# Mixture-of-experts stage of a fused attention and expert layer: another order of shared units, zero rows, gathers and down rows

## The reference, cut to what matters

```python
scores = softmax(xt @ gate_w.T)                       # 8 experts
idx = top_k(scores + gate_b, 2)[1]
cw = sum(one_hot(idx, 8) * weights[..., None], axis=1)
h1 = einsum('td,efd->etf', xt, w1) + b1[:, None, :]
h3 = einsum('td,efd->etf', xt, w3) + b3[:, None, :]
y = einsum('etf,edf->etd', swiglu(h1 * h3), w2) + b2[:, None, :]
routed = einsum('te,etd->td', cw, y)
shared = swiglu((xt @ sw1.T + sb1) * (xt @ sw3.T + sb3)) @ sw2.T + sb2
return routed + shared
```

## Time and profile before

| | us |
|---|---|
| median of 3 runs | 1384.94 |
| lowest and highest | 1378.19, 1387.31 |
| the profiled execution's own time | 1380.67 |
| its span | 1378.8 |
| mean granted TensorE clock | 0.909 |
| attention | 0 to about 980 |
| experts | about 980 to 1378.8 |

### The profile page before, as it was taken

One profiled execution on the slowest core, in us unless ns is written; L12 is line 12 of the kernel. 1 busy time (PEld: TensorE's weight loads), 2 busy tenths in 40 slices (PEclk: granted clock), 3 DMA queues, 4 the chain that ended last, 5 costly groups with the idle time before them and its releaser, 6 DMA issues. The chain is left out here.

```text
span 1378.8 us, 22331 instructions
## 1 busy us (share of the span) xinstructions
PE 1133.1 (82%) x6568; PEld 475.6 (34%) x6568; DVE 1094.1 (79%) x2499; ACT 943.7 (68%) x1748; POOL 833.1 (60%) x1129
## 2 busy tenths in 40 slices
PE   2599999999998998999999899984599987887710
PEld 0122222232232232222222222222478866665510
DVE  2589999999999899989899998933567755999734
ACT  1028888787786886877778678783489975777511
POOL 5254366565675776667567575556378525887555
PEclk9559999999998999999899999997699998999955
DMA  2361242242241431423323224002224443444312
GB/s 65 82 187 50 56 102 63 50 109 55 65 117 40 104 87 51 112 56 79 78 63 102 70 58 110 19 26 91 68 87 153 146 145 108 138 135 144 95 33 76
DMA packets 104009, 119.89 MB, mean 87 GB/s; under 512 B 13217, under 2 KB 80965, under 8 KB 103621
## 3 DMA queue, kind: packets, MB, share of 16 engines
q1 hardware_dynamic: 93728, 97.55, 26.2%
q0 software_dynamic: 8192, 16.79, 4.4%
q10 hardware_dynamic: 1968, 4.13, 0.8%
HBM read 58.91 MB, written 59.51 MB: 86 GB/s over the span
## 5 line engine op out<-in xcount | busy, mean ns | idle before, releaser
L929 DVE TENSOR_REDUCE MX<-psS 128x1 f32<-128x512 f32 x1024 | 652.9, 679 | 71.5 <-PE psS L423 62.7
L678 ACT ACTIVATE PR<-psST 128x512 f32<-128x512 f32 x986 | 536.8, 600 | 166.0 <-PE psST L411 153.2
L423 PE MATMUL psS<-KS,QS 48*128 48x512 bf16 x1024 | 368.0, 408 | 51.9 <-DVE MX L929 27.2
L411 PE MATMUL psST<-QS,KS 51*128 51x512 bf16 x986 | 337.2, 393 | 22.0 <-ACT PR L678 8.1
L437 PE MATMUL psPV<-PR,V 128*32 128x512 f32 x2048 | 283.0, 625 | 7.1 <-ACT OT L592 2.0
L411 PEld LDWEIGHTS psST<-QS,KS 51*128 51x128 bf16 x986 | 76.4, 93 | 382.3 <-ACT PR L678 323.7
L1703 POOL DMA_INDIRECT GOT<-scratch_y,FROM x128 | 128.8, 1007 | 38.4 <-issue 35.9
L423 PEld LDWEIGHTS psS<-KS,QS 48*128 48x128 bf16 x1024 | 84.5, 94 | 114.0 <-DVE MX L929 87.9
L1033 POOL DMA_INDIRECT scratch_x<-XN,POSI x96 | 95.3, 993 | 27.8 <-issue 27.4
L1060 POOL TENSOR_TENSOR ROT<-ROT,RES 128x512 f32<-128x512 f32 x32 | 40.5, 1267 | 91.2 <-DVE RES L737 91.2
L1378 PE MATMUL psH<-XH,WS 128*128 128x512 f32 x184 | 82.5, 448 | 10.3 <-DVE XL L1532 7.6
(11 more groups left out here) (173 smaller groups left out, 2016.7 us busy)
## 6 DMA issues: line engine op xcount, KB each, us to landing
scratch_parts<-PT SPq DMA_DIRECT2D x192, 128.0 KB
QS<-scratch_parts SPq DMA_DIRECT2D x64, 192.0 KB, 3.4
KS<-scratch_parts SPq DMA_DIRECT2D x64, 192.0 KB, 4.5
XR<-scratch_x SPq DMA_DIRECT2D x46, 256.0 KB
scratch_y<-YR SPq DMA_DIRECT2D x46, 256.0 KB
scratch_x<-ZERO SPq DMA_DIRECT2D x18, 256.0 KB
X<-in_x SPq DMA_DIRECT2D x16, 256.0 KB, 4.9
scratch_turned<-XT SPq DMA_DIRECT2D x16, 256.0 KB, 4.6
```

The costliest lines, as they stand in the source:

```text
L411: nc.tensor.matmul(bank(st_banks(t), k)[:], KS[t.par][rows, h // 2, kc * P:(kc + 1) * P], QS[t.par][rows, h // 2, :], start=True, stop=Tru ...
L423: nc.tensor.matmul(bank(psS, k)[:], QS[b.par][rows, h // 2, qc * P:(qc + 1) * P], KS[b.par][rows, h // 2, :], start=True, stop=True).then_ ...
L678: nc.scalar.activation(PR[:, s % 2, j, :], bank(st_banks(t), k)[:], ACT.Exp, scale=SCALE).then_inc(st_exp, 1)
L929: nc.vector.tensor_reduce(out=MX[:, qc, h:h + 1], in_=bank(psS, k)[:], axis=AX.X, op=ALU.max).then_inc(s_max, 1)
```

## The change

1. **Order.** Stream two carries a shared unit only after its third, sixth and ninth routed unit (`MIXED` = 3: S4 to S6 in slots 34, 38 and 42). R45 moves from slot 55 to slot 52, and nine shared units S7 to S15 fill slots 53 to 61. `GATHER_AT` of stream two becomes slot 56. `FINISH` is 37, 39, ... 49 for batches 0 to 6 and 56, 58, 60, 62, ... 72 for batches 7 to 15.
2. **Zero rows.** The eight tiles are written one at a time at slots 0, 3, ... 21, ahead of the slot's store, and no longer wait for stream two's scatters.
3. **Down rows.** POOL's copy of 128x132 is gone; SP copies the same rows from WD to DS by a DMA (`load_down(p + 2)`, between `store_rows(p - 2)` and `load(p + 3)`), with a register load of the expert's number, for each of the 46 routed units. PE and ACT wait for its landing.
4. **POOL.** `rsqrt` of a finished batch comes between the second and the third gather of its slot.
5. **Buffers and slots.** YR gets three buffers instead of two, R(b) twelve instead of eight (the third four are XN2). `shift` and `scale` come at +4, `residual` at +6 and ahead of `weigh`, `store_out` at +7.

```diff
-        R_BUFS = 2 * QC
+        R_BUFS = 3 * QC
+        MIXED = 3
+        Y_BUFS = 3
...
-            if i % 3 == 2:
+            if i % 3 == 2 and i < 3 * MIXED:
                 ORDER.append(("S", next(shared)))
...
-        FINISH = [GATHER_AT[int(b >= SPAN)] + (GATHERS * (b - FIRST_B[int(b >= SPAN)] + 1)) // PACE + 1 for b in range(B)]
-        END = max(FINISH) + 6
+        FINISH = []
+        for b in range(B):
+            st = int(b >= SPAN)
+            soonest = GATHER_AT[st] + GATHERS * (b - FIRST_B[st] + 1) // PACE + 1
+            FINISH.append(max(soonest, SLOT_S[b] + LAG + 1, FINISH[-1] + 2 if b else 0))
+        END = max(FINISH) + 8
...
+            def load_down(i):
+
+                if i == 0:
+                    sp.wait_ge(halved, 1)
+                if i in FIRST_UNIT:
+                    sp.wait_ge(expert_ready, FIRST_UNIT.index(i) + 1)
+                if i >= D_BUFS:
+                    sp.wait_ge(y_psum, SLOT_R[i - D_BUFS] + 1)
+                    sp.wait_ge(gl_ready, 2 * (SLOT_R[i - D_BUFS] + 1))
+                e = sp.value_load(EXPERT[0:1, i:i + 1], min_val=0, max_val=NE)
+                sp.dma_start(DS[:, i % D_BUFS], WD[:, bass.ds(e, 1)].rearrange("p e c -> p (e c)")
+                             ).then_inc(down_loaded[i % D_BUFS], 16)
+
...
-            def zero_tails():
-                for i in range(4):
-                    sp.wait_ge(scattered[i], SCATTERED[1][i] * 16 * GATHERS)
-                sp.wait_ge(count_ready, 1)
-                for e in range(NE):
-                    row = sp.value_load(CNTI[0:1, e:e + 1], min_val=ROOM * e, max_val=ROOM * e + SPAN * N)
...
+            def zero_tail(e):
+                if e == 0:
+                    sp.wait_ge(count_ready, 1)
+                row = sp.value_load(CNTI[0:1, e:e + 1], min_val=ROOM * e, max_val=ROOM * e + SPAN * N)
...
             for p in range(END):
-                if p == SLOT_R[UNITS[0]] - 6:
-                    zero_tails()
+                if p % 3 == 0 and p // 3 < NE:
+                    zero_tail(p // 3)
                 if routed(p - LAG):
                     store_rows(p - LAG)
+                if routed(p + 2):
+                    load_down(ORDER[p + 2][1])
                 load(p + 3)
-                if p - 6 in FINISH:
-                    store_out(FINISH.index(p - 6))
-            store_out(B - 1)
+                if p - 7 in FINISH:
+                    store_out(FINISH.index(p - 7))
...
                 if routed(p):
-                    pe.wait_ge(ds_ready, ORDER[p][1] + 1)
+                    pe.wait_ge(down_loaded[ORDER[p][1] % D_BUFS], 16 * (ORDER[p][1] // D_BUFS + 1))
...
                 if routed(p):
-                    if i >= 2:
-                        act.wait_ge(y_stored[i % 2], 16 * (i // 2))
-                    place = YR[:, i % 2]
+                    if i >= Y_BUFS:
+                        act.wait_ge(y_stored[i % Y_BUFS], 16 * (i // Y_BUFS))
+                    place = YR[:, i % Y_BUFS]
...
-                if p - 3 in FINISH:
-                    scale(FINISH.index(p - 3))
+                if p - 4 in FINISH:
+                    scale(FINISH.index(p - 4))
...
+                if p - 6 in FINISH:
+                    residual(FINISH.index(p - 6))
                 if p in FINISH:
                     weigh(FINISH.index(p))
-                if p - 5 in FINISH:
-                    residual(FINISH.index(p - 5))
...
-            def stage(i):
...
-                nc.gpsimd.tensor_copy(DS[:, i % D_BUFS], WD[:, bass.ds(e, 1)].rearrange("p e c -> p (e c)")).then_inc(ds_ready, 1)
...
+            def gathers(p, first, last):
+                for st in range(STREAMS):
+                    n = PACE * (p - GATHER_AT[st])
+                    if 0 <= n < (SPAN, B - SPAN)[st] * GATHERS:
+                        for i in range(first, last):
+                            gather(FIRST_B[st] * GATHERS + n + i)
...
-                if routed(p + 2):
-                    stage(ORDER[p + 2][1])
...
+                gathers(p, 0, PACE // 2)
                 if p - 2 in FINISH:
                     rsqrt(FINISH.index(p - 2))
+                gathers(p, PACE // 2, PACE)
```

More of the change, by code:

```diff
@@ L1208, in experts @@
         HA = sb("HA", [P, HA_BUFS, N], F32)
-        YR = sb("YR", [P, 2, QC, C], F32)
+        YR = sb("YR", [P, Y_BUFS, QC, C], F32)
         GOT = sb("GOT", [P, G_BUFS, TOPK, QC, C], F32)
@@ L1241, in experts @@
         y_psum, y_evicted = sem("y_psum"), sem("y_evicted")
-        y_stored = [sem(f"y_stored{i}") for i in range(2)]
-        ws_act, ds_ready = sem("staged_by_act"), sem("down_staged")
+        y_stored = [sem(f"y_stored{i}") for i in range(Y_BUFS)]
+        ws_act, down_loaded = sem("staged_by_act"), [sem(f"down_loaded{i}") for i in range(D_BUFS)]
         gathered = [sem(f"gathered{i}") for i in range(G_BUFS)]
@@ L1251, in R @@
         def R(b):
+            if b % R_BUFS >= 2 * QC:
+                return XN2[:, b % QC]
             half = (W1, W3)[b % R_BUFS // QC][:].rearrange("p e f -> p (e f)")
@@ L1287, in load_rows @@
                     "(p q) c -> p q c", q=QC)).then_inc(xr_loaded[i % X_BUFS], 16)
-            def zero_tails():
-                for i in range(4):
-                    sp.wait_ge(scattered[i], SCATTERED[1][i] * 16 * GATHERS)
-                sp.wait_ge(count_ready, 1)
-                for e in range(NE):
-                    row = sp.value_load(CNTI[0:1, e:e + 1], min_val=ROOM * e, max_val=ROOM * e + SPAN * N)
-                    sp.dma_start(XG[1][bass.ds(row, TILE), :].rearrange("(p q) c -> p q c", q=QC),
-                                 ZERO[:].rearrange("p (q c) -> p q c", q=QC)).then_inc(zero_filled, 16)
+            def zero_tail(e):
+                if e == 0:
+                    sp.wait_ge(count_ready, 1)
+                row = sp.value_load(CNTI[0:1, e:e + 1], min_val=ROOM * e, max_val=ROOM * e + SPAN * N)
+                sp.dma_start(XG[1][bass.ds(row, TILE), :].rearrange("(p q) c -> p q c", q=QC),
+                             ZERO[:].rearrange("p (q c) -> p q c", q=QC)).then_inc(zero_filled, 16)
             def load_turned(b):
@@ L1439, in hidden @@
                 if gl == 0 and routed(p):
-                    act.wait_ge(ds_ready, ORDER[p][1] + 1)
+                    act.wait_ge(down_loaded[ORDER[p][1] % D_BUFS], 16 * (ORDER[p][1] // D_BUFS + 1))
                 if due(2 * p + gl - 3):
@@ L1455, in evict @@
                 if routed(p):
-                    if i >= 2:
-                        act.wait_ge(y_stored[i % 2], 16 * (i // 2))
-                    place = YR[:, i % 2]
+                    if i >= Y_BUFS:
+                        act.wait_ge(y_stored[i % Y_BUFS], 16 * (i // Y_BUFS))
+                    place = YR[:, i % Y_BUFS]
                 else:
-                    if i < R_BUFS:
+                    if i < 2 * QC:
                         act.wait_ge(split, min(2 * (i % QC) + 3, EXP_ALL))
+                    elif i < R_BUFS:
+                        act.wait_ge(scattered[i % QC], SCATTERED[1][i % QC] * 16 * GATHERS)
                     else:
@@ L1635, in _ @@
                         clip(p, 0)
-                if p - 3 in FINISH:
-                    shift(FINISH.index(p - 3))
+                if p - 4 in FINISH:
+                    shift(FINISH.index(p - 4))
                 if 0 <= p - 1 < ALL:
@@ L1698, in gather @@
                     pool.wait_ge(from_step, 4 * (st + 1))
-                    for i in range(2):
-                        pool.wait_ge(y_stored[i], 16 * ((FIRST_UNIT[st] + UNITS[st] + 1 - i) // 2))
+                    for i in range(Y_BUFS):
+                        pool.wait_ge(y_stored[i], 16 * len(range(i, FIRST_UNIT[st] + UNITS[st], Y_BUFS)))
                 if rest == 0 and b >= G_BUFS:
@@ L1725, in _ @@
                     scatter(2 * p + 1)
-                for st in range(STREAMS):
-                    for n in range(PACE * (p - GATHER_AT[st]), PACE * (p - GATHER_AT[st] + 1)):
-                        if 0 <= n < (SPAN, B - SPAN)[st] * GATHERS:
-                            gather(FIRST_B[st] * GATHERS + n)
+                gathers(p, 0, PACE // 2)
                 if p - 2 in FINISH:
                     rsqrt(FINISH.index(p - 2))
+                gathers(p, PACE // 2, PACE)
 def build(nc, x, wqkvT, chan, ones, cos, sin, perm, ident, table, count, gate_wT, gate_b, w1T, w3T, wdT, b2, out):
```

8 lines of the change are left out of this document (1 added, 7 removed).

## The result

The changed kernel took 1399.68 us in the median of four runs (1397.55 to 1404.26), beside 1384.25 us (1378.19 to 1387.31) of the kernel before. The ratio is 1.0106, with a 95% interval from 1.0062 to 1.015. The forecast was 1357: the sign was wrong. Ratios and intervals leave out disturbed runs, one of e7 (1716.48 us) and the two longest of e17.

A forecast was written before the change was run, and what follows sets the result against it. PE was taken to bound stream one, DVE's list batches 0 to 6, POOL's 48 gathers the end. Zero rows -8.3, down rows +4, batch 10's gathers from 1271.5, plus 67.4, 16.5 and 1.9 around the span: 1357 us, range 1336 to 1377.

The forecast's parts named there:

- stretch (c): From the first gather to the weighing of batch 0: 30.6 us, partly unexplained, kept as long as it was.
- Rival B: A long stand like the 17.7 us falls into the new end and costs POOL 12 us: 1369; chance 0.20.
- Rival A: ACT's unexplained waits, if from POOL's copy or a buffer, go too, shortening the first-gather stretch by about 14: 1343; chance 0.25.
- Rival C: SP's list becomes the bound of stream one; at 5 us a copy, 45 more: 1402; chance 0.07.
- Rival D: The order only moves work; 4.3 from the zero tiles and 3 or so are left: 1374; chance 0.08.
- Zero rows: Stream one: spreading the eight zero tiles closes the eviction hole, -8.3 us, with bounds of -8.3 and -6.
- Down rows by DMA: Stream one: the copy lengthens SP's list between store and XR load, +4 us, with bounds of 0 and 13.
- POOL's copy gone: POOL falls from 12.2 to about 11.4 us a batch, hidden by PE and DVE: 0, with bounds 0 and -7.5.
- (d): From batch 0's weighing to batch 6's: 68.34 us, 11.4 a batch, with DVE's own list as the bound.
- changes nothing else here: POOL's root moved between gathers was taken to have no other effect, being not late until the end.
- Order: Stream two: batch 7 weighed in slot 56, so batch 10's gathers start at 1271.5, not 1289.0.
- The end: POOL's last 48 gathers take 67.4 us, at 11.5 a batch later on, then 16.5 us follow the last gather.

The follow-up runs named there:

- e7: Changed kernel with POOL made to wait once a slot for PE's y signal before its gathers: 0.9919 of the kernel before.
- e17: Changed kernel without the 24 gathers of batches 0 to 2, run where signals were late: 1376.27 us, 0.9904 of the kernel before.
- e6: Kernel before, nothing edited, run again where no signal was late: 1365.58 us, 1.0004.
- e18: Changed kernel, nothing edited, run where signals were late: 1397.45 us beside 1385.99 for the kernel before, 1.0078.
- e5: Changed kernel, nothing edited, run where no signal was late: 1348.15 us beside 1365.42 for the kernel before, 0.9875.
- e16: Changed kernel with XR's load ahead of the down rows on SP and due shared batches finished a slot earlier, signals late: 1386.81 us, 1.0003 of the kernel before.
- e10: Changed kernel with POOL's copy of the down rows back, second run, no late signals: 1343.97 us, 0.9815 of the kernel before.
- e15: Changed kernel with POOL's copy of the down rows back, third run, no late signals: 1347.7 us, 0.9875 of the kernel before.
- e4: Changed kernel with the old order, a shared unit after every third routed one to the end: 1352.49 us, 0.9901 of the kernel before.
- e1: Kernel before with only its zero rows spread over the slots: 1356.8 us beside 1365.96, 0.9931.
- e2: Changed kernel with POOL's copy of the down rows back in place of SP's DMA: 1348.96 us, 0.9876 of the kernel before.
- e12: Kernel before with its down rows copied by DMA on SP and nothing else changed: 1364.16 us beside 1365.84, 0.9986.
- e3: Changed kernel with XR's load issued ahead of the down rows' copy on SP: 1342.45 us, 0.9827 of the kernel before.
- e8: Changed kernel with XR's load ahead of the down rows on SP and due shared batches finished one slot earlier: 1340.51 us, 0.9823 of the kernel before.
- the fifth set: Later runs with late signals: changed kernel unedited 1397.45 us, without 24 gathers 1376.27, load first and batches earlier 1386.81, beside 1385.99 for the kernel before.

## Why the prediction was wrong, point by point

The forecast was a list of stretches, so it can be laid beside five traces. All numbers are differences of rows: the starts of POOL's first gather, of the weighings of batches 0 and 6, of POOL's first gather of batch 10 and of its last one, and the end of the span. (The forecast counted to the end of the last gather, 67.4 and 16.5; the table takes its start, 0.95 earlier.)

| us | before | e6 (before) | forecast | after | e18 (after) | e5 (after) |
|---|---|---|---|---|---|---|
| late signals | yes | no | | yes | yes | no |
| first gather at | 1142.4 | 1135.6 | 1138.1 | 1148.5 | 1144.1 | 1138.0 |
| to weighing 0 | 30.6 | 18.5 | 30.6 | 42.0 | 43.2 | 18.8 |
| to weighing 6 | 68.3 | 73.4 | 68.3 | 82.7 | 83.1 | 65.3 |
| to batch 10's first gather | 47.7 | 50.4 | 34.5 | 39.9 | 37.3 | 35.9 |
| to the last gather | 74.9 | 65.3 | 66.4 | 71.2 | 70.6 | 70.6 |
| to the end | 14.9 | 15.0 | 17.5 | 18.1 | 18.1 | 18.1 |
| span | 1378.8 | 1358.2 | 1355.4 | 1402.5 | 1396.4 | 1346.7 |

*The step that failed* is the one at stretch (c): "I keep stretch (c) as long as it was, since I can't explain it". 12 of its 30.6 us were late signals (30.6 beside 18.5 in e6), and they don't stay as long when the work around them changes. In the changed kernel POOL doesn't wait for PE before a copy, its gathers come in one run of 22 where there had been 16 and a stand, and the same stretch became 42.0; the next one, which I carried over as "68.3 us later", became 82.7. These two are 25.8 us of the 47.1 between forecast and trace. 10.4 more lie ahead of the first gather, some 8 of them in the attention, and the rest behind batch 6. Where no signal is late (e5) the same two stretches were 11.8 and 3.0 us shorter than forecast, and the span 8.7 shorter.

What the state with late signals costs in all can be read across a row pair: the kernel before is 1378.8 - 1358.2 = 20.6 us longer in it, the changed kernel 1396.4 - 1346.7 = 49.7. The attention, which is the same in both, has 7.2 and 8.7 of these (its end moves by as much without late signals: 974 to 981 us); `experts` alone has 13.4 and 41.0. The medians say the same: 1384 and 1386 us beside 1365 to 1366 for the kernel before, 1397 to 1400 beside 1348 to 1350 for the changed one. The 29 us between the two costs are more than the 17 that the change gains by the medians where signals are in time (1348.15 against 1365.42). That is the sign of the result. Which part of the change makes the state dearer isn't shown: of the versions only e16 and e17 ran in it.

*Rival B* named the condition ("Both stands fall into long unbroken runs of gathers (16 and 24), and the change makes such runs, 22 at the start"), and e17 shows that the gathers at the start were one cause: 21 to 24 us. Its price was wrong. I gave it the 12 us that POOL lost before, at the end; it came at the start, where DVE, PE and POOL all stood behind it, and not in the end, where the trace after has no signal over 2.5 us late from 1302 on. So a long run of gathers isn't enough by itself: batches 10 to 15 are gathered in one there, broken by roots alone. Whether the length of a run, its lead over PE, or something else makes a signal late is open. e7, e10 and e15 were to show it and fell into sets without late signals.

*Rival A* said that ACT's stands might go, for 1343. Where they are gone the changed kernel's span is 1346.7. But its reason, a copy or a buffer, is refuted: e6 has both and no stand. Its price had a slip besides: from 30.6 us to 12.3 and 2 are 16 us less, not 14.

*Rival C* gave 1402, and 1399.68 was measured: that is luck. C wanted a copy that holds SP's queue for 5 us, and slots of stream one over 4.6 us. The copy took 1.3 us there and the slots 4.46, no longer than where no signal was late (4.457 in e5).

*Rival D* said that the order only moves work. By e4 it is worth 2 to 4 us, so D was near for the order alone; its 1374 left out what the other parts brought.

*Zero rows*, -8.3: right (e1: -9.2, 7.0 to 7.2 of them in stream one), and the hole is closed in the trace after as well.

*Down rows by DMA*, +4 with bounds of 0 and 13: the mechanism was right, and the term was mis-sized. "I take 0.3 us for two slots": it was 0.28 for one, 7.3 us in stream one by e2 and 7.4 by e12. The 1.2 us that I called free weren't all free: a load issued 1.29 us later behind its store made each slot 0.28 longer, where (1.29 - 1.2) / 2 would be 0.05. By the Trainium skill ("DMA: Bandwidth & Descriptors", Issuing engines are not separate DMA queues) the time to initiate a DMA "is usually small relative to the DMA itself"; here it was 1.1 to 1.3 us of SP for a copy and the term was 7.3 us, of which e3 took 6.6 away by order alone.

*POOL's copy gone*, "I take 0": wrong. In e6, where nothing is late, the stretch between weighings 0 and 6 is 73.4 / 6 = 12.2 us a batch, POOL's own 12.2. My (d) took DVE's own list for the bound because the trace before had 11.4 there and no wait of DVE for POOL; but that stretch began behind late signals, and POOL, which went on with its gathers under them, may have had a lead in it. In e6 DVE waits for POOL's roots there, from 1154 to 1228 us:

```profile
DVE SH L1619 <- POOL RS L1715: 7.1, 5, 1.6
```

Two parts of the change end these waits. e12 takes away nothing but the copies: 68.6 us, and 2.4 us of such waits. e2 has everything but that: 68.5, and none. Both together have 65.3 / 6 = 10.9 a batch (e5). Neither the zero rows nor the order has a part in it (73.5 in e1, 65.2 in e4). So the copies are worth 3 to 5 us in this stretch, which is why part 3 comes out even, and parts 4 and 5 as much again. The two weren't tested apart, but what ends is a wait for the root, and part 4 moved the root: "changes nothing else here" was wrong too.

*Order*: batch 10's first gather was to come 17.5 us earlier and to be limited by the weighing of batch 7. Both held without late signals: 19.9 us (1277.94 to 1258.06), and the row's releaser is DVE's weighing. But it isn't the order's work alone: with the order undone (e4) the gather comes at 1265.13, so the order brings 7.1. The last gather is 9.2 us earlier by it (1337.86 to 1328.65), and the tail behind it 4.6 longer than in e4. Against the kernel before the tail is 3.1 longer (18.1 after 15.0), where I had 2.5, and by the mechanism that I gave: two weighings start behind the last gather in e5 (1331.71 and 1335.90), one in e6 (1347.44).

*The end*: 67.4 us for 48 gathers, measured 71.5 (70.6 to the start of the last). I counted 11.5 us a batch; with the root between the gathers it is 12.0, and the first three batches no longer run through without one (65.3 in e6).

A word on the profiles: the two on record are 23.7 us apart, their medians 15.4. The attention before the experts, which no edit touches, ended 8.4 us later in the changed kernel's profiled run (POOL's scaling of WD starts at 989.6, not 981.2).

## What to carry to other kernels

A wait that the profile can't explain is a term of its own, not part of the stretch it lies in: carry it with a range of its own size, and compare the two kernels in more than one set of runs, since the sign may hang on it. On a queue that is near its limit, put the transfer that someone waits for ahead of a new one: that alone was 6.6 us here (e3 against e5, by the ratios). The version with both edits of e8 was 0.9823 of the kernel before where signals were in time, level with e3 as the best that held, and 1.0003 where they were late.

## What the runs showed of the hardware that was not expected

In the traces of the first two runs and of the fifth set, PE's signals come late while POOL issues gathers. From the start of the last matmul into psY to its eviction it is 0.31 us in the median of every trace, but up to 19.6 (before), 24.4 (after), 22.7 (e18), 23.4 (e16) and 9.9 us (e17, with 24 gathers fewer). In the fifteen traces of e1 to e15 the most is 4.1 us, in slot 1, and one of 3.5 to 4.1 us is there in all traces.

In the trace after, updates of four of PE's semaphores that by the modelled ends of their matmuls were due between 1156 and 1166 us all come between 1179.78 and 1180.04, while POOL's gathers have gone on landing in between. An update of ACT in the same stretch is in time: 1163.58, where its instruction ends at 1163.57. So it is PE's side that is held. The longest late signals end 3.6 to 4.0 us after the issue of the run's last gather has ended (after, before, e16, e18). The 22 gathers are needed for the long one (e17), but gathers don't suffice: slots 53 to 61 of the changed kernel have gathers and no late signal.

The same state shows in the attention, and there too POOL issues indirect transfers back to back, eight scatters from 920.49 to 930.45 us in the trace after. PE's four transposes for DVE's reciprocal end at 926.40 there, and at 921.48 in e5, which has the eight scatters as well. DVE's reciprocal in the trace after and in e5:

```profile
929.16 0.26 DVE L714 RECIPROCAL REC<-psM 128x16 f32<-128x16 f32 x1 [8.11 <-remote]
```

```profile
921.52 0.26 DVE L714 RECIPROCAL REC<-psM 128x16 f32<-128x16 f32 x1 [5.38 <-PE psM L445]
```

It starts 2.7 to 2.8 us behind the transposes in each of the five traces, and 0.04 in e5 and e6. The attention ends at 981 to 990 us in the five, and at 974 to 981 in e1 to e15. What puts a set of runs into this state wasn't found.
